# First row-maximum step of the pair two ahead: at the end of the full-array phase instead of ahead of the scores

## The reference, cut to what matters

```python
q = layernorm(x) @ Wq * scale;  k, v = split(media @ Wkv)            # 16 heads of 64
sim = where(media_mask, einsum('bhid,bhjd->bhij', q, k), neg_inf)
x = x + tanh(attn_gate) * (einsum('bhij,bhjd->bhid', softmax(sim), v) @ Wo)
x = x + tanh(ff_gate) * (gelu(layernorm(x) @ W1) @ W2)
mp = einsum('bme,de->bmd', media, W_mem)                              # second layer
c = softmax(x @ mp.T / sqrt(256)) @ mp
x = rmsnorm(x + sigmoid(concat(x, c) @ W_gate + b_gate) * c)
```

## Time and profile before

| | |
|---|---|
| median of 3 runs | 901.36 us (900.8 to 902.85) |
| span of the profiled execution | 897.9 us (its time in all is not listed apart) |
| PE busy | 849.0 us, 95% |
| DVE busy | 592.1 us, 66% |
| ACT busy | 460.7 us, 51% |
| POOL busy | 397.7 us, 44% |

### The profile page before, as it was taken

One profiled execution on the slowest core, in us unless ns is written; L12 is line 12 of the kernel. 1 busy time (PEld: TensorE's weight loads), 2 busy tenths in 40 slices (PEclk: granted clock), 3 DMA queues, 4 the chain that ended last, 5 costly groups with the idle time before them and its releaser, 6 DMA issues.

```text
span 897.9 us, 18267 instructions
## 1 busy us (share of the span) xinstructions
PE 849.0 (95%) x7811; PEld 709.2 (79%) x7811; DVE 592.1 (66%) x955; ACT 460.7 (51%) x724; POOL 397.7 (44%) x180
## 2 busy tenths in 40 slices
PE   3789999999999999999999999999999999999987
PEld 2478878888878888888888888888887778888775
DVE  6666688867848888677588886756787612043363
ACT  3465555656635556575356665735554441234352
POOL 2155555555645556566256565663566550000000
PEclk9699999999999999999999999999999999999999
DMA  9000001000000010000000000000001500001100
GB/s 273 24 1 1 1 1 38 1 2 1 2 1 1 1 38 2 1 1 2 1 2 1 1 1 2 1 2 1 1 2 39 166 1 0 1 1 37 38 24 23
DMA packets 19842, 16.67 MB, mean 19 GB/s; under 512 B 930, under 2 KB 18739, under 8 KB 19763
## 3 DMA queue, kind: packets, MB, share of 16 engines
q1 hardware_dynamic: 19474, 15.25, 5.8%
q10 hardware_dynamic: 288, 0.27, 0.1%
HBM read 14.46 MB, written 1.05 MB: 17 GB/s over the span
## 4 chain that ended last, share of the span: by engine, by line
PE 78%; DVE 12%; ACT 5%; issue 2%; POOL 1%; DMA 1%; POOLq 0%; DVEq 0%
PE psum L1239 21%; PE psum L1253 16%; PE psum L338 14%; PE psum L1204 6%; PE psum L1162 3%; PE psum L1268 3%; PE psum L1017 3%; PE psum L1031 3%; PE psum L1104 3%; DVE mx L871 2%; DVE k_lo L860 2%; DVE ot L901 1%; PE psum L1259 1%; POOL acc L435 1%; ACT k_hi L591 1%
## 5 line engine op out<-in xcount | busy, mean ns | idle before, releaser
L435 POOL TENSOR_TENSOR acc<-acc,ring 128x1024 f32<-128x1024 f32 x128 | 306.6, 2396 | 18.7 <-POOL acc L435 0.5
L871 DVE TENSOR_REDUCE mx<-psum 128x2 f32<-128x800 f32 (+2 forms) x256 | 245.5, 990 | 88.4 <-PE psum L1204 80.6
L614 ACT ACTIVATE ring<-psum 128x1024 f32<-128x1024 f32 x192 | 196.8, 1026 | 67.6 <-PE psum L1239 61.0
L430 POOL TENSOR_TENSOR acc<-ring 128x1024 f32<-128x1024 f32 x32 | 76.6, 2394 | 283.9 <-ACT ring L614 283.9
L1253 PE MATMUL psum<-ring,v 128*64 128x256 f32 (+1 forms) x1664 | 186.7, 381 | 1.7
L1253 PEld LDWEIGHTS psum<-ring,v 128*64 128x64 f32 (+1 forms) x1664 | 116.7, 137 | 61.0 <-DVE k_lo L860 3.8
L1239 PE MATMUL psum<-nm,maskrow 64*128 64x256 f32 (+1 forms) x832 | 124.1, 294 | 0.6 <-ACT ring L614 0.6
L1239 PE MATMUL psum<-q_hi,k_hi 64*128 64x256 f32 (+1 forms) x832 | 117.3, 278 | 0.0
L1239 PE MATMUL psum<-q_lo,k_hi 64*128 64x256 f32 (+1 forms) x832 | 117.0, 277 | 0.0
L1239 PE MATMUL psum<-q_hi,k_lo 64*128 64x256 f32 (+1 forms) x832 | 117.0, 277 | 0.0
L608 ACT COPY od<-psum 128x512 f32<-128x512 f32 x32 | 18.8, 587 | 172.3 <-PE psum L1259 172.3
(11 more groups left out here) (151 smaller groups left out, 1371.2 us busy)
## 6 DMA issues: line engine op xcount, KB each, us to landing
nat<-in_ctx_dram SPq DMA_DIRECT2D x8, 768.0 KB
w<-in_L_xattn_W_dram SPq DMA_DIRECT2D x2, 1024.0 KB, 8.1
ring<-in_L_xattn_Wkv_dram SPq DMA_DIRECT2D x2, 512.0 KB, 10.1
wq<-in_L_xattn_Wq_dram SPq DMA_DIRECT2D x1, 1024.0 KB, 10.2
wo<-in_L_xattn_Wo_dram SPq DMA_DIRECT2D x1, 1024.0 KB, 11.1
out_dram<-t_res SPq DMA_DIRECT2D x8, 128.0 KB, 1.8
mask<-in_mask_BxS_bk_dram SPq DMA_DIRECT2D x4, 200.1 KB, 6.9
xs<-in_x_dram SPq DMA_DIRECT2D x3, 256.0 KB, 6.7
```

The lines of the kernel that those rows point to most:

```text
L430: nc.gpsimd.tensor_tensor(acc[:, :, :, :], ring[:, 0, :, :, :], ring[:, 1, :, :, :], ALU.add)\
L435: nc.gpsimd.tensor_tensor(acc[:, :, :, :], acc[:, :, :, :], ring[:, g, :, :, :], ALU.add)\
L614: nc.scalar.activation(ring[:, g, :, :, :], score_set[m % 2].rearrange("p (h i q) -> p h i q", h=2, i=2), ACT.Exp).then_inc(S["p_ready"], 1)
L871: nc.vector.tensor_reduce(mx[:, t, :, c], pair[:, :, 0:min(c1, KEYS) - c0], axis=AX.X, op=ALU.max).then_inc(S["m_max"], 1)
```

## The change

The item M(j+2, 0) is put at the end of `full_phase(j)`, behind R(j+1), instead of M(j+1, 0) at the head of `row_phase(j)`. In a row phase the order becomes M1, S0, M2, S1, and so on. Since the bank counter starts at 1 now, M still has aligned pairs; the tail's tiles move to other banks, and three of its waits with them.

```diff
 def row_phase(j):
-    out = [("M", j + 1, 0), ("S", j, 0), ("M", j + 1, 1)]
-    for g in range(1, KEY_GROUPS):
+    out = []
+    for g in range(KEY_GROUPS):
         out += [("M", j + 1, g + 1), ("S", j, g)]
     return out
...
-    return out + [("F", j - 1), ("R", j + 1)]
+    return out + [("F", j - 1), ("R", j + 1), ("M", j + 2, 0)]
...
-        table, n = {}, 0
+        table, n = {}, 1
...
-        turn_psum = [score_set[1][:, 0:512], score_set[1][:, 512:1024], aux[0], aux[1]]
-        gate_psum, wmt_psum = score_set[0], aux[3][:, 256:512]
-        first_hidden = psum[:, 2560:3584]
+        turn_psum = [score_set[1][:, 0:512], score_set[1][:, 512:1024], aux[1], aux[1]]
+        gate_psum, wmt_psum = score_set[0], aux[1][:, 256:512]
+        first_hidden = psum[:, 3072:4096]
...
                 elif i == 2:
-                    upto(pe, "od_in", BATCH - 1, PAIRS - 1)
+                    pe.wait_ge(S["wmt_ready"], 1)
+                    upto(pe, "nm_in", BATCH - 1, PAIRS)
                 else:
-                    pe.wait_ge(S["ff_gelu"], 1)
+                    pe.wait_ge(S["ff_zt"], 3)
...
                     elif kind == "O":
-                        if order is LAST:
-                            pe.wait_ge(S["ff_gelu"], 1)
                         upto(pe, "ot_ready", b, PAIRS)
```

More of the change, by code:

```diff
@@ L272, in cross_attention_kernel @@
         lane_bank = [[lane_psum[lane][:, 512 * i:512 * (i + 1)] for i in range(4)] for lane in range(LANES)]
-        assert BANK["A", 6] == 0 and BANK["A", 7] == BANK["R", 7] == 3 and BANK["O", 0] == 2
-        turn_psum = [score_set[1][:, 0:512], score_set[1][:, 512:1024], aux[0], aux[1]]
-        gate_psum, wmt_psum = score_set[0], aux[3][:, 256:512]
-        first_hidden = psum[:, 2560:3584]
+        assert BANK["A", 6] == BANK["A", 7] == BANK["O", 0] == 0 and BANK["R", 7] == 1
+        turn_psum = [score_set[1][:, 0:512], score_set[1][:, 512:1024], aux[1], aux[1]]
+        gate_psum, wmt_psum = score_set[0], aux[1][:, 256:512]
+        first_hidden = psum[:, 3072:4096]
         ff2_psum = [aux[2], aux[3], aux[2], aux[3]]
```

## The result

| | before | after |
|---|---|---|
| median | 902.11 us (900.8 to 903.49, 4 runs) | 918.43 us (916.85 to 920.15, 4 runs) |
| span of the profiled execution | 897.9 | 918.3 |
| PE busy | 849.0 us, 95% | 853.9 us, 93% |

The ratio is 1.0185 (1.0165 to 1.0204): 16.3 us slower. Forecast were 916 and a range of 908 to 922. The changed kernel's profiled execution is its slowest run: 920.15 us around a span of 918.3, so 1.8 us lie around the span. So the two traces differ by 20.4 us where the medians differ by 16.3.

The account below looks back on a forecast made before the run. PE's own stream was taken to bound the attention part (busy 98.68 of 100 us). Adding 31.2 us between R and A and 1.0 at the start, less 17.25 gained, gave +14.9 on 901.4: 916 us, range 908 to 922.

Parts of the forecast that it names:

- The steady sum: All terms behind the first order, waits and turns added less gains in row phases and handovers: forecast +13.95 us.
- R to A: From the full-array transpose to the column phase: M0 waits for just-filled banks, then turns; +31.2 us over 30 pairs.
- The turn: M0's slot with the change of tile shape before the column phase: 0.39 us, bounds 0.29 to 0.53.
- The hiding of A's first load under M0: Column phase's first weight load pulled ahead under M0: turn about 0.28, sum 2.9 us less; not taken.
- The row phase: Without M0 at its head each row phase shortens by 0.33 to 0.44, taken as 0.40: 12.0 us gained, phases of 7.87.
- The late maxima: Seven row phases where DVE is still busy when M0 is ready: 2.2 of 2.4 us gained.
- Handover and D: At batch handovers M0's wait for ACT's copy goes, 3.05 us gained; D stays covered, without waiting for U's fold.
- The faster rival: Bank waits already met when M0 arrives, only turns remain: -4.4 us, 897.0; chance 5%.
- a wait of A9: With j = 9 the column phase itself waits for K.3's bank: +0.91 us in four pairs.
- The first order: Kernel start: changed bank waits for T, K, V and M.9.1, taken as +1.0 us, from -1 to +3.
- that of M.9.1: In the first order M.9.1 takes M.9.0's banks and waits for its maximum: +0.8 us.
- What lies around the span: Time of an execution outside its profiled span: 3.5 us, the median 901.36 less the span 897.9.

Follow-up runs that it names:

- Experiment 3: The changed kernel with M0 at its new place but writing to a free score set, out of the bank rotation: 896.67 us, 0.9942 of the kernel before.
- experiment 2: The changed kernel with a V behind the last K in odd full phases too: 917.86 us, 1.0179 of the kernel before.
- experiment 9: The changed kernel with M.9.0 of the first pass in a score set: 916.41 us, 1.0146 of the kernel before.
- experiment 10: The changed kernel with M.9.0 of the first pass in a score set and the banks of K.8.2 and K.8.3 exchanged: 913.88 us, 1.012.
- experiment 1: The changed kernel with two first-order key chunks' banks exchanged, so K.8.3 and not K.8.2 waits for G.4's bank: 917.22 us, 1.0172 of the kernel before.
- experiment 7: The kernel before with M2 one step later (order M0 S0 M1 S1 M2 M3 S2): 918.7 us, 1.0197 of the kernel before.
- experiment 8: The kernel before with M2 one step later and a POOL memset of 128x384 ahead of each pair's first add: 899.25 us, 0.9962.
- experiment 5: The kernel before with two first-order key chunks' banks exchanged, so K.8.2 waits for G.4's bank: 904.11 us, 1.0016 of the kernel before.
- experiment 6: The kernel before with V last in every full phase: 903.03 us, 1.0007 of the kernel before.
- experiment 4: The kernel before with M0 left at the row phase's head but in a free score set, M1 right behind it: 893.96 us, 0.9912.

## Why the prediction was right, and where it wasn't

*The steady sum.* +14.1 against +13.95 is closer than its terms are: R to A costs 0.7 more than forecast, and the full phases, put at nothing, give back 0.6 for a reason that no run here shows. That these two cancel is luck.

*R to A.* Right in mechanism and size: +31.9 measured, +31.2 forecast. M0 waits for what the last chunk holds: k_lo ends at R+1.31 in odd pairs, as read from the earlier trace rows. M0 follows 0.10 behind, where I had taken 0.06 to 0.07. That trifle is the 0.03 between 1.78 and 1.75, and 1.07 and 1.05. Experiment 3 takes the banks away and with them 23.3 us; experiment 2 moves the last chunk and M0 with it.

*The turn.* 0.38, taken as 0.39 from the earlier trace rows. Experiment 3 shows it alone, without a wait before it, so it does not lie in the wait's shadow. Of the two pages of the Trainium skill that I weighed, the rule on TensorEngine Tiling (Array Packing), section Key Properties, that changing the tiling mode drains the engine, agrees with the trace: the slot is 0.38. The hiding of A's first load under M0, 0.28, for which I had read the Trainium skill's page TensorE: Matmul & The Clock Gate, section Architectural detail, does not appear in any of the 26 pairs, nor with free banks; the load starts with A, 0.37 behind M0.

*The row phase.* 7.87 to 7.89 in 27 of 30, forecast 7.87. The late maxima gave 2.4, forecast 2.2 (the one with 0.53 went from 8.79 to 7.87, and the last from 9.57 to 8.49).

*Handover and D.* -3.1 as forecast; D to M 0.53 at all four; D without a wait.

*The faster rival* was rightly improbable for this kernel, and its arithmetic holds: with banks that are free M0 stands at R+0.27 and A at R+0.65 as it had said. Experiment 3 is that rival made real, 4.7 us faster than before where it gave 4.4. That nearness is luck: two of its terms don't hold there and cancel. It counted a wait of A9 (0.91 in four pairs, 0.2 there) and the handover's gain of 3.05, which experiment 3 doesn't have.

*The first order is the term that was mis-sized*: +1.0 forecast, from a range of -1 to +3; +6.3 in the profiled execution, and about +2.2 in the medians (16.3 less the steady 14.1). The waits that I read from the bank table came out small up to V.4.0 (+0.7 forecast, +0.2 measured: 36.55 against 36.37), and that of M.9.1 near its forecast (+0.8, measured 1.09). What I sized wrongly is PE's clock: a late rise, 4.1 us in this pair of traces, and a second fall after M.9.1's wait, 2.2. I had written that the clock "may rise sooner or later" and gave it no more than 2 us; 10 us at the lower level do the work of 5 at the upper. The second fall belongs to the change: the three traces with both waits of the two M have it, and experiments 9 and 10 undo it. The late rise isn't shown to: experiment 1 takes away the wait that was blamed and the clock still rises late, and experiments 7 and 8 differ by as much with the same instructions. Experiments 9 and 10 have the first steady R within 0.6 to 1.3 us of before, one trace each.

*What lies around the span.* I took 3.5 us (median less span); it is 1.8, and the profiled execution was simply one of the kernel's faster runs. This moves nothing in the steady terms, since they are differences, but it is why two single traces must not be read as the difference of two medians.

*Open.* The second fall is tied to the two M of pair 9 by experiments 9 and 10, but they changed M.9.0's bank and two waits at once. When the clock rises between 40 and 50 us differs also where M0 isn't moved at all (granted clock 0.82, 0.65, 1.00 and 0.53 in experiments 5 to 8). The runs on record show that this is largely the execution and not the kernel: of the 42 runs of the kernel before beside the experiments, the 16 that took 899.59 to 901.44 us have a mean granted clock of 0.988 to 0.990, and the 26 that took 902.19 to 903.84 have 0.985 to 0.987. As an estimate from these numbers, 0.003 less over 900 us is 5.4 us more at 1.2 instead of 2.4 GHz, in which 2.7 us are lost; the two groups lie 2.8 apart. Only one execution of this kernel has a trace, so where the slower ones lose the time isn't shown. On its page TensorE: Matmul & The Clock Gate, Part 1: The HAM clock gate, the Trainium skill says that the number of slow matmuls at a kernel's start varies between runs of one kernel; the two groups agree with it. What decides between an early and a late rise stays open.

## What to carry to other kernels

Before an in-order engine's instruction is moved into the place just behind a phase's last products, list the banks that it takes and who empties them last: that date, more than the instruction's own slot, is the price, and it is paid by everything queued behind (23.3 of 31.9 us here). If the idle to be filled is a wait for a result, look for a free bank first: experiment 4 got more that way than the move did with free banks (6.3 us of the steady part against 4.3). And after any change of order look at the durations of the short operations in the chain as well as their order: a shift of 0.4 us was worth 19. Last, don't read the start of a kernel from one trace each: two with the same instructions there lay 4.2 us apart.

## What was not expected of the hardware

- A VectorE operation of 226 ns (128x128, float32 to fp32r, from SBUF to SBUF) took 2166 ns in the median when it started 0.3 us after a GpSimd add, and ended 0.08 us behind that add. Started 0.01 to 0.06 us ahead of an add, it took 226. Shifting GpSimd's adds by 0.4 us brought it back to 227 (experiments 7 and 8). On its page SBUF — State Buffer, section SBUF: two separate sides, the Trainium skill calls the port pair that VectorE and GpSimd share an exclusive lock, held for a whole instruction; the trace agrees, with 2.15 us beside an add of 2.4.
- PE's clock fell a second time in the middle of busy work, from 56.74 us on, 1.4 us behind a wait of 1.09 us that had followed one of 1.24. It did not where only one such wait stood there: 1.24 at 49.69 before, 1.24 at 53.38 in experiment 8, 0.90 at 51.34 in experiment 9.
- The clock rose at about 40 us in one execution and at about 49 in another, in kernels with the same instructions until then (experiments 7 and 8).
- A matmul in 64*128 tiles between full-array and 128*64 work costs 0.38 us until the next starts, whether or not it waited first (1.06 us of idle or none).
